# Block matrices for the stream mixing, residual rows added by VectorE, Sinkhorn iterations written out: the last stage of a two-layer kernel

## What is computed

```python
H_res = sinkhorn_log(H_res_logits)          # 50 iterations on one 4 x 4 matrix per token
H_pre, H_post = softmax(H_pre_logits), softmax(H_post_logits)
g = sigmoid(gate)[0]
H_res = (1.0 - g) * I + g * H_res
x_pre = einsum('btnc,btn->btc', x_streams, H_pre)
y = x_pre @ W_branch
x_mixed = einsum('btij,btjc->btic', H_res, x_streams)
y_distributed = einsum('btc,btn->btnc', y, H_post)
out = residual + x_mixed + y_distributed     # x_streams: the layer-normed residual
```

## Time and profile before

| | us |
|---|---|
| median of 3 runs | 1069.11 (1068.39 to 1069.32) |
| the profiled execution, its own time | 1068.61 |
| its span in the trace | 1066.8 |
| outside the span | 1.8 |

### The profile page before, as it was taken

One profiled execution on the slowest core, in us unless ns is written; L12 is line 12 of the kernel. 1 busy time (PEld: TensorE's weight loads), 2 busy tenths in 40 slices (PEclk: granted clock), 3 DMA queues, 4 the chain that ended last, 5 costly groups with the idle time before them and its releaser, 6 DMA issues. The chain is left out here.

```text
span 1066.8 us, 20481 instructions
## 1 busy us (share of the span) xinstructions
PE 1027.7 (96%) x7316; PEld 784.7 (74%) x7320; DVE 870.0 (82%) x1880; ACT 663.7 (62%) x1130; POOL 93.6 (9%) x85
## 2 busy tenths in 40 slices
PE   9999999999999999999999999999999999946968
PEld 7988889777777777777777777776888887524637
DVE  6854444899999999999999999965764995979998
ACT  5332220699999989899989988953231114635826
POOL 0310101200000000000000000000011112400000
PEclk9999999999999999999999999999999999977989
DMA  9477779923113333212333321167315000000003
GB/s 360 153 267 258 284 233 274 331 61 75 40 42 74 74 69 74 67 33 52 74 74 69 74 55 35 41 235 246 119 60 172 0 0 1 1 1 0 1 1 157
DMA packets 55857, 112.96 MB, mean 106 GB/s; under 512 B 7756, under 2 KB 21196, under 8 KB 55676
## 3 DMA queue, kind: packets, MB, share of 16 engines
q1 hardware_dynamic: 55740, 112.26, 34.3%
q0 software_dynamic: 64, 0.00, 0.0%
HBM read 83.99 MB, written 27.26 MB: 104 GB/s over the span
## 5 line engine op out<-in xcount | busy, mean ns | idle before, releaser
L960 DVE CUSTOM_DVE_ANT_0 XS<-b_psS,b_mbias 128x1024 f32<-128x1024 f32 x256 | 311.1, 1215 | 0.6 <-PE b_psS L838 0.3
L915 ACT ACTIVATE XS<-XS,b_mins 128x1024 f32<-128x1024 f32 x256 | 295.8, 1155 | 9.7 <-DVE b_mins L960 9.2
L871 PEld LDWEIGHTS b_psT<-ident,XS 128*128 128x128 f32 x2048 | 230.0, 141 | 65.8 <-issue 47.6
L871 PE MATMUL b_psT<-ident,XS 128*128 128x128 f32 x2048 | 271.9, 276 | 1.7 <-ACT b_PT L923 1.7
L969 DVE COPY b_PT<-b_psT 128x512 f32<-128x512 f32 x256 | 176.9, 691 | 27.0 <-PE b_psT L871 25.3
L923 ACT COPY b_PT<-b_psT 128x512 f32<-128x512 f32 x256 | 149.5, 584 | 39.1 <-PE b_psT L871 31.0
L838 PE MATMUL b_psS<-XTh 128*128 128x512 f32 x512 | 155.9, 422 | 0.8 <-PEq L115 0.7
L852 PE MATMUL b_psO<-b_PT,XTh 128*32 128x256 f32 x1984 | 132.8, 385 | 0.0
L838 PEld LDWEIGHTS b_psS<-XTh 128*128 128x128 f32 x512 | 85.1, 189 | 18.4 <-DVE b_mins L960 7.4
L852 PEld LDWEIGHTS b_psO<-b_PT,XTh 128*32 128x32 f32 x1984 | 51.8, 109 | 42.1 <-issue 20.8
L468 ACT ACTIVATE a_oh<-a_psM 128x512 fp32r<-128x512 f32 x24 | 14.2, 595 | 99.5 <-PE a_psM L371 93.0
(11 more groups left out here) (284 smaller groups left out, 1647.6 us busy)
## 6 DMA issues: line engine op xcount, KB each, us to landing
XS<-in_ctx SPq DMA_DIRECT2D x16, 512.0 KB, 5.6
XTh<-QHd SPq DMA_DIRECT2D x32, 256.0 KB, 4.8
XTh<-QLd SPq DMA_DIRECT2D x32, 256.0 KB, 5.4
XS<-in_ctx_turned SPq DMA_DIRECT2D x8, 512.0 KB, 8.0
XS<-in_x SPq DMA_DIRECT2D x8, 512.0 KB, 11.3
a_wst<-in_L_xattn_w_q SPq DMA_DIRECT2D x8, 512.0 KB, 5.4
a_xn<-in_ctx_turned SPq DMA_DIRECT2D x8, 512.0 KB, 4.2
QHd<-a_oh SPq DMA_DIRECT2D x16, 256.0 KB, 4.3
```

Source lines behind the costliest of these rows:

```text
L871: last_t = pe.transpose(psT[:, kt, :], Pr[:, k % PR, kt * P:(kt + 1) * P], ident[:])
L915: act.activation(Pr[:, k % PR, :], Sc[:, k % 4, :], ACT.Exp, bias=mins[:, k % 4:k % 4 + 1], scale=-1.0, accum_out=sums[:, u, j:j + 1]).the ...
L960: dve.tensor_tensor_reduce(out=Sc[:, k % 4, :], in0=psS[:, k % 2, :], in1=mbias[:, qt, :], scale=1.0, scalar=3.4e38, op0=ALU.add, op1=ALU.min,
```

## The change

Tokens are put on partitions in another way for the mixing. A tile's 128 tokens are cut into four groups of TG = 32. `XNg` holds, for a group g of a tile, stream n of the group's 32 tokens on partitions 32n to 32n + 31; 32 DMAs of 128 KB, from 32 partitions of `XN` to 32 partitions of `XNg`, fill it (SP, once four tiles of `XN` are there, and again once all eight are). `Hd[:, t, g]` is a 128 x 128 matrix with 16 diagonal blocks of 32 x 32 that carry `H`; with it as weights one product of 256 columns mixes all four streams of 32 tokens. 32 such products do the mixing; nothing is accumulated.

To make `Hd`, 16 small products with slices of `ident` move `H` into a bank `psH` with the stream on the partition group, and DVE multiplies it, spread out, by `block_ident`, 8 instructions of 128 x 512. `block_ident` is summed from `ident` by DVE ahead of the Sinkhorn iterations. `post_sum` turns the rows into the same form, with 32 products of 32 output partitions in place of 4 of 128; `rowterm` is turned too (`row_g`, 16 small products and a copy), and `keep_sum` is four activations in place of one. The mixed halves of a tile go to 7 banks in turn, and DVE adds each, 128 x 512, to `XR`: 16 instructions. DVE's own mixing, the diagonals `dg`, the residual rows put into banks ahead of `H`, and ACT's copies are gone.

`XR` then has stream i on partitions 32i to 32i + 31, so a store is 32 partitions with pieces of 256 numbers (1 KB): 24 stores in place of 8, for the first four tiles two tiles at a time (256 KB, SP), for the others one tile at a time (128 KB; SP streams 0 and 1, ACT streams 2 and 3). The 49 Sinkhorn iterations are written out with no loop.

```diff
-        PER_LOOP, LOOPS = 7, (1, 3, 3)
+        ROUNDS = (7, 21, 21)
+        NEAR = 4
+        TG = P // STREAMS
+        QB = 7
+        NQ = 2 * NT
...
+        def store(engine, t, tiles, i):
+            rows = out[t * P:(t + tiles) * P, stream(i)].rearrange("(g r) c -> r g c", r=TG)
+            engine.dma_start(rows, XR[group(i), t:t + tiles, :].rearrange("r t (g c) -> r (t g) c", c=CH)
+                             ).then_inc(out_done, 16)
...
         @block.sync
-            for t in range(NT):
-                sp.wait_ge(mixed, MIX * t + (STREAMS - pe_rows(t)) * STREAMS)
-                sp.wait_ge(rows_kept, t + 1)
-                sp.dma_start(out[t * P:(t + 1) * P, :], XR[:, t, :]).then_inc(out_done, 16)
+            for t in range(0, NT, QT):
+                sp.wait_ge(pre_spread, t + QT)
+                for n in range(STREAMS):
+                    for g in range(STREAMS):
+                        sp.dma_start(XNg[group(n), t:t + QT, g, :], XN[group(g), t:t + QT, stream(n)]
+                                     ).then_inc(streams_in, 16)
+            for t in range(0, NT, 2):
+                both = t < QT
+                if not both:
+                    wait_half(sp, 2 * t + 1)
+                    for i in range(2):
+                        store(sp, t, 1, i)
+                if both:
+                    wait_half(sp, 2 * t + 2)
+                wait_half(sp, 2 * t + 3)
+                for i in range(STREAMS if both else 2):
+                    store(sp, t if both else t + 1, 1 + both, i)
...
         @block.tensor
             def post_sum(t):
-                for rows, ready in ((XR[:, t, :], None), (yp[:, t % 2, :], post_scaled)):
...
+                def part(g, rows, first):
+                    for i in range(STREAMS):
+                        last = pe.matmul(psD(t % 2)[group(i), g * CH:(g + 1) * CH], ident[:, group(g)], rows[:, stream(i)],
+                                         start=first, stop=not first)
+                    return last
...
-            pe.wait_ge(sink, LOOPS[2])
-            for t in range(NT):
-                pe.matmul(psZ[t][:, 0:pe_rows(t) * CH], ident[:], XR[:, t, (STREAMS - pe_rows(t)) * CH:],
-                          start=True, stop=False)
...
+            pe.wait_ge(streams_in, 16 * STREAMS * STREAMS * (NT // QT))
+            pe.wait_ge(sink, 2)
+            by_stream = H[:].rearrange("p t (i n) -> p n t i", n=STREAMS)
+            for g in range(STREAMS):
                 for n in range(STREAMS):
-                    for i in range(rows):
...
+                    last = pe.matmul(psH[group(n), g, :, :], ident[:, group(g)], by_stream[:, n, :, :], start=True, stop=True)
+            last.then_inc(spread, 1)
+            for q in range(NQ):
+                t, u = divmod(q, 2)
+                if u == 0:
+                    pe.wait_ge(sink, t + 3)
+                if q >= QB:
+                    wait_half(pe, q - QB)
+                for g in (2 * u, 2 * u + 1):
+                    last = pe.matmul(psZ[q % QB][:, g % 2 * CH:(g % 2 + 1) * CH],
+                                     Hd[:, t, g, :, :].rearrange("p i r -> p (i r)"), XNg[:, t, g, :],
+                                     start=True, stop=True)
                 last.then_inc(mixed_pe, 1)
...
         @block.vector
+            dve.tensor_reduce(block_ident[:], ident[:].rearrange("p (n r) -> p r n", n=STREAMS), AX.X, ALU.add
+                              ).then_inc(lg, 1)
...
+            dve.wait_ge(spread, 2)
+            dve.wait_ge(lg, 9)
             for t in range(NT):
-                mix(t)
+                dve.tensor_tensor(Hd[:, t], psH[:, :, t, :].unsqueeze(3).to_broadcast([P, STREAMS, STREAMS, TG]),
+                                  block_ident[:].unsqueeze(1).unsqueeze(1).to_broadcast([P, STREAMS, STREAMS, TG]),
+                                  ALU.mult).then_inc(sink, 1)
+            dve.wait_ge(post_added, NT)
+            for q in range(NQ):
+                dve.wait_ge(mixed_pe, q + 1)
+                dve.tensor_tensor(kept_half(q), psZ[q % QB], kept_half(q), ALU.add).then_inc(rows_added, 1)
```

More of the change, by code:

```diff
@@ L2058, in post_sum @@
                     pe.wait_ge(post_added, t - 1)
-                for rows, ready in ((XR[:, t, :], None), (yp[:, t % 2, :], post_scaled)):
[L2060 to L2064, removed]
+                def part(g, rows, first):
[3 more added lines that the diff above has]
+                    return last
+                for g in range(0, STREAMS, 2):
+                    part(g, XR[:, t, :], True)
+                pe.wait_ge(post_scaled, t + 1)
+                for g in range(0, STREAMS, 2):
+                    part(g, yp[:, t % 2, :], False)
+                    part(g + 1, XR[:, t, :], True)
+                    last = part(g + 1, yp[:, t % 2, :], False)
                 last.then_inc(post_mm, 1)
+            for g in range(STREAMS):
+                for i in range(STREAMS):
+                    last = pe.matmul(psR[group(i), g, :], ident[:, group(g)], rowterm[:], start=True, stop=True)
+            last.then_inc(spread, 1)
             pre_stream(0)
@@ L2126, in keep_sum @@
                 act.wait_ge(post_mm, t + 1)
-                act.activation(XR[:, t, :], psD(t % 2), ACT.Identity, bias=rowterm[:, t:t + 1]).then_inc(post_added, 1)
+                for g in range(STREAMS):
+                    cols = slice(g * CH, (g + 1) * CH)
+                    last = act.activation(XR[:, t, cols], psD(t % 2)[:, cols], ACT.Identity, bias=row_g[:, g, t:t + 1])
+                last.then_inc(post_added, 1)
+            act.wait_ge(spread, 1)
+            act.copy(row_g[:], psR).then_inc(exps, 1)
+            act.wait_ge(exps, 5)
             act.wait_ge(soft_step, 4)
@@ L2139, in _ @@
                 keep_sum(t)
[L2141 to L2164, removed]
+            for t in range(QT, NT):
+                wait_half(act, 2 * t + 1)
+                for i in range(2, STREAMS):
+                    store(act, t, 1, i)
         @block.vector
@@ L2221, in _, with iterations @@
             col_step(1)
-            def iterations(loops, n, near=None):
-                with dve.Fori(0, loops):
-                    for i in range(PER_LOOP):
-                        if near is not None and i == 2:
-                            dve.sem_inc(near, 1)
-                        row_step(n + i * 2 * STEP)
-                        col_step(n + i * 2 * STEP + STEP)
-                    dve.sem_inc(chain, -2 * STEP * PER_LOOP)
+            def iterations(rounds, n, near=None):
+                for i in range(rounds):
+                    if near is not None and i == rounds - NEAR:
+                        dve.sem_inc(near, 1)
+                    row_step(n + i * 2 * STEP)
+                    col_step(n + i * 2 * STEP + STEP)
+                return n + rounds * 2 * STEP
             n = STEP + 1
-            iterations(LOOPS[0], n)
+            n = iterations(ROUNDS[0], n)
             dve.wait_ge(soft_step, 3)
@@ L2250, in _ @@
             n += 5 * CHAINS
-            iterations(LOOPS[2], n, sink)
+            n = iterations(ROUNDS[2], n, sink)
             times(n, 3, ra, T, M)
```

69 lines of the change are left out of this document (32 added, 37 removed).

## The result

| | before | after |
|---|---|---|
| median, us | 1069.11 (5 runs: 1068.39 to 1070.42) | 1064.0 (5 runs: 1062.94 to 1064.33) |
| ratio | | 0.9954, 95% interval 0.9943 to 0.9965 |
| the profiled execution: its time, its span | 1068.61, 1066.8 | 1063.93, 1062.1 |
| a mark in stage e before the iterations (start of `e_zc`) | 950.04 | 950.88 |
| end of `H` | 1036.67 | 1035.35 |

The change makes the kernel 5.1 us faster by the medians, 4.9 us (0.46%) by the ratio, and takes it to 1064.0 where 1068.6 was forecast. The span fell by 4.7 us: 2.16 us between the mark and `H`, 3.38 us after `H`, less 0.84 us by which the mark itself came later.

A forecast was written before the change was run, and what follows sets the result against it. Bound by the path of Sinkhorn iterations, `H`, DVE's mixing and one store; -1.9 (iterations) + 0.3 (`block_ident`) + 1.4 (`H` to the end, stores binding) = -0.2 us, forecast 1068.6 us, range 1060 to 1072.

The forecast's parts named there:

- The rival with ACT's stores beside SP's: Final stores: ACT's queue overlaps SP's fully for the last four tiles, leaving 15.0 us in line; 1063.4 us, chance 0.12.
- iterations written out: Sinkhorn iterations ahead of `H`: removing loop turns, entries and exits saves 1.9 us.
- `block_ident`: DVE between row maxima and first Sinkhorn step: making it adds 0.3 us, with nothing to hide it.
- first store after `H`: Start of the final stores: the first waits for half 3 and is issued 9.7 us after `H`.
- 4.19 MB of stores: Final stores: all output leaves from 32 partitions at a time at 210 GB/s, taking 20.0 us.
- `H` to the end: From `H` to the span's end: 9.7 + 20.0 + 1.8 = 31.5 us against 30.1 before, +1.4.
- The branch: PE and ACT work beside the iterations: some 6 us longer over 8 tiles, 4.3 us a `post_sum`, but hidden.
- From `H` to the last addition: Mixing after `H`: 18.9 us in place of 27.0, PE ending later than DVE by 1.2 us.
- The products on `H`: 16 small PE products after `H`, and back to DVE: taken as 2.3 us, between under 1 and 4.3.
- The loads alternate between the four quarters on one queue, and gain nothing by it: Final stores: ground for 210 GB/s, taken from stage a's loads into 32 partitions each.
- not held by the 32 partitions: Final stores: reads differ from writes and go at 347 GB/s; 1060.5 us, chance 0.20.
- the one with both handicaps multiplied: Final stores: small pieces and 32 partitions together give 182 GB/s, 23.0 us of data; 1071.6 us, chance 0.12.

The follow-up runs named there:

- loops_back: The changed kernel with the three hardware loops of the Sinkhorn iterations put back (1, 3 and 3 turns of 7); 1065.08 us, ratio 0.9971.
- two_queues: The changed kernel with streams 0 and 1 of all tiles stored on SP's queue, 2 and 3 on ACT's, from the first store on; 1059.66 us.
- same_half: The changed kernel, but for the last four tiles SP stores streams 0 and 2, ACT 1 and 3; 1063.2 us, ratio 0.9946.
- warm_pe: The changed kernel with 24 extra unused PE products ahead of `H`, to have PE's clock up when mixing starts; 1063.3 us, ratio 0.9955.
- all_rows_1k: The changed kernel with 8 stores of 128 partitions, still in 1 KB pieces, output permuted (a probe, no candidate); 1059.29 us, ratio 0.9911.
- sp_only: The changed kernel with all stores on SP's queue in the same pieces, ACT issuing none; 1064.26 us, ratio 0.9958.
- interleaved_warm: warm_pe, with DVE making `Hd` of three tiles, then alternating a tile's two sums and one `Hd`; 1062.16 us, ratio 0.9939.
- all_three: two_queues joined with the edits of interleaved_warm, with 28 extra PE products in place of 24; 1059.1 us, ratio 0.9914.
- all_three_paced: all_three with the extra PE products paced by DVE's last four iterations, and 3 more before the first `Hd`; 1058.69 us, ratio 0.9909.

## Why the prediction was right or wrong

The time lies inside the range (1060 to 1072), and the forecast itself was 4.6 us too high. It gave no change its largest chance, 0.43, and "faster" 0.40; the kernel became faster, below the 1067.0 at which that begins. The rival with ACT's stores beside SP's gave 1063.4 and 26.5 us from `H` to the end, against 1064.0 and 26.75 measured; its number was right, its reason mostly not, so that it came out is mostly luck. The rivals' times start from two bases: 1060.5 and 1063.4 from 1068.6, but 1071.6 and 1070.5 from 1068.8, 0.2 us too high; nothing hangs on it. Term by term:

| term | forecast | measured |
|---|---|---|
| iterations written out | -1.9 | -1.8 and -2.0 by ratios, -1.8 and -2.4 from the mark to `H` |
| `block_ident` | +0.3 | +0.1 |
| first store after `H` | 9.7 | 8.7 |
| 4.19 MB of stores | 20.0 (210 GB/s) | 16.35 (257) |
| issue to first data, and last data to the end of the span | 1.8 | 1.7 |
| `H` to the end | 31.5 | 26.75 |

**The loops** were right in place and, within 0.5 us, in size, from the row of one turn. **`block_ident`** was put wholly on the path. It took 0.35 us, but the first step began 0.35 us after `e_mx` where it had been 0.26 before: most of it fell into DVE's wait for ACT's `M`, which the forecast had seen and given no credit.

**The branch** was right: hidden, though 64 narrow records cost 3.6 us a tile and not 4.3. `XNg` landed long before it was wanted.

**From `H` to the last addition** 18.9 us were forecast and 19.0 came, out of two errors that cancel; that sum was luck. The products on `H`, the one piece without a row, took 0.90 us with both hops, not 2.3; the working had named "under 1 us" as the low end. And the half clock lasted 6.7 us after the restart where some 3 were taken from the earlier trace rows. In the kernel before PE had then worked in one piece; here the small products and a gap of 0.8 us came first. That this is the cause isn't shown: with the same products and the same gap it lasted 4.7 us in `loops_back`, 4.9 in `two_queues` and 7.5 in `same_half`. Neither mattered to the end, but the first moved the first store: 1.4 us sooner by the products, 0.4 of which was lost again in the additions ahead of it.

**The step that failed is the rate of the stores.** That they and not the additions bind was right (`warm_pe`), and that the 32 partitions and not the 1 KB pieces hold them (`all_rows_1k`), and also the 210 for the start: 194 to 218 GB/s while one half is worked on. Wrong was "The loads alternate between the four quarters on one queue, and gain nothing by it", carried over from loads to stores. On one queue the stores moved 244 (`sp_only`), 2.8 us of the 3.65; ACT's queue gave the other 0.8. Why loads into 32 partitions stayed at 210 with the same alternation is open: they went the other way, in pieces of 2 and 4 KB, and with PE's and ACT's work around them; no run here separates these.

The rival "not held by the 32 partitions" (0.20) is refuted, the one with both handicaps multiplied too: the piece's handicap doesn't add to the partitions'.

## What to carry to other kernels

When a layout puts what must be stored on a quarter of the partitions, price the store by what such transfers move in the trace, and then ask which two of them run side by side: the same stores on two queues gave 312 GB/s with one half of the partitions to each queue, and 259 with both in one half. An engine that the chain names last, and even a clock at half speed in it, can be free: `warm_pe` ended the additions 2.7 us sooner and the kernel no sooner, because the stores had long been behind. And a term with no row at all (the products on `H`, 0.90 us) was over-priced by its neighbours of 256 columns; 32 records of 32 columns took 0.69 us at half clock.

## What was not expected of the hardware

- A single queue isn't bound to the rate of one half all the time: 244 GB/s in the mean (`sp_only`) against 194 to 218 while its first two stores, in one half, run. An overlap of consecutive stores in different halves would fit.
- Two queues reach 312 GB/s from 32 partitions each, in 1 KB pieces, if the pairs lie in different halves.
- PE's clock, at 1.00 while the branch ran, stood at 0.50 for 6.7 us after the restart in the changed kernel, against 3.3 in the kernel before (1027.42 to 1030.7), and between 4.7 and 7.5 in kernels with the same products after `H`. In `interleaved_warm` it was up during the extra products and at 0.50 again after 1.8 us without work and 0.67 us of narrow products; in `all_three`, with 0.80 us without work ahead of `H`'s products, and in `all_three_paced`, with 0.5, it stayed at 1.00.
